# Audio tower on one core: three hand-written orders and the PSUM banks are replaced

## What is computed

```python
h = _L0_tok_ref(x, L0_tok_W, L0_tok_b)
h = h + _L0_attn_ref(_layernorm(h), ...)
    # dots = q k^T / 8; attn = softmax(dots); attn = einsum('bhij,hg->bgij', attn, reattn_w)
    # attn = layernorm over the head axis * ln_g + ln_b; out = (attn v) w_out^T + b_out
h = h + _L0_ffn_ref(_layernorm(h), ...)
    # scores = softmax(x gate^T); the two largest, normalised, weigh relu(x w1 + b1) w2 + b2; plus a shared expert
```

## Time and profile before

| | us |
|---|---|
| median of 3 runs | 638.5 (638.1 to 639.48) |
| the profiled execution: its time | 639.33 |
| the profiled execution: its span | 637.5 |
| PE busy | 606.4 (95%) |
| VectorE busy | 441.2 (69%) |
| ScalarE busy | 402.4 (63%) |
| GpSimd busy | 368.5 (58%) |

### The profile page before, as it was taken

How to read it: one execution, slowest core, us unless ns; L and a number is a source line. 1 busy time by engine, 2 the same in 40 slices (tenths; PEclk the granted TensorE clock), 3 DMA queues, 4 the chain that set the end, 5 groups by cost and what they waited for, 6 DMA issues and landing times.

```text
span 637.5 us, 17017 instructions
## 1 busy us (share of the span) xinstructions
PE 606.4 (95%) x6275; PEld 529.2 (83%) x6275; DVE 441.2 (69%) x1322; ACT 402.4 (63%) x1346; POOL 368.5 (58%) x545
## 2 busy tenths in 40 slices
...
DMA packets 15460, 37.43 MB, mean 59 GB/s; under 512 B 1809, under 2 KB 4241, under 8 KB 15377
## 3 DMA queue, kind: packets, MB, share of 16 engines
...
## 4 chain that ended last, share of the span: by engine, by line
PE 75%; ACT 7%; DVE 7%; POOL 5%; issue 3%; DMA 1%; SPq 0%; ACTq 0%; POOLq 0%; DVEq 0%
PE ps_fill L414 13%; PE ps_fill L416 11%; PE ps_fill L415 11%; PE ps_mix L642 9%; PE ps_dots L630 9%; PE ps_av L650 7%; PE ps_fill L778 6%; PE ps_fill L570 4%; ACT ex L803 3%; DVE aT L1086 3%; POOL sum L1227 2%; PE ps_fill L770 2%; ACT sq L811 2%; POOL sum L1230 1%; PE ps_fill L761 1%
## 5 line engine op out<-in xcount | busy, mean ns | idle before, releaser
L803 ACT ACTIVATE ex<-ps_dots,negmax 128x92 f32<-128x92 f32 x384 | 123.7, 341 | 7.0 <-DVE negmax L1070 6.5
L1227 POOL TENSOR_TENSOR sum<-sq 92x384 f32<-92x384 f32 x64 | 64.2, 1003 | 80.3 <-ACT sq L811 79.5
L1221 POOL TENSOR_TENSOR probs<-ex,rinv 128x552 f32<-128x552 f32 x64 | 71.0, 1109 | 29.7 <-DVE rinv L1076 29.7
L642 PE MATMUL ps_mix<-mixk,probs 64*92 64x64 f32 x1536 | 79.2, 251 | 5.5 <-DVE aT L1086 5.4
L642 PEld LDWEIGHTS ps_mix<-mixk,probs 64*92 64x92 f32 x1536 | 70.7, 163 | 16.3 <-issue 10.7
L1167 DVE SCALAR_TENSOR_TENSOR act<-ps_fill,b_neg,spread 128x368 f32<-128x368 f32 x123 | 67.9, 591 | 19.9 <-PE ps_fill L416 15.1
L803 ACT ACTIVATION_READ_ACCUMULATOR ex<-ps_dots,negmax 128x1 f32 x384 | 81.4, 212 | 0.0
L630 PE MATMUL ps_dots<-xT,yT 128*64 128x92 f32 x1536 | 75.6, 249 | 5.5 <-ACT ex L803 4.9
L630 PEld LDWEIGHTS ps_dots<-xT,yT 128*64 128x64 f32 x1536 | 65.0, 139 | 11.6 <-ACT ex L803 8.8
L1086 DVE TENSOR_TENSOR aT<-ps_mix,arstd 92x384 f32<-92x384 f32 x128 | 64.9, 547 | 7.1 <-ACT arstd L821 5.2
L1244 POOL TENSOR_TENSOR xT<-xT_split_hi,xT_split_lo 128x368 f32<-128x368 f32 x16 | 15.6, 973 | 86.1 <-DVE xT_split_lo L1146 86.1
...
## 6 DMA issues: line engine op xcount, KB each, us to landing
...
```

The lines of the kernel that those rows point to most:

```text
L642: last = pe.matmul(ps_mix[0:N, half, DH * c:DH * c + DH], probs[rows, (s - 1) % 2, c, :], mixk[rows, :, :].rearrange("p g i -> p (g i)"), ...
L803: last = act.activation(ex[:, s % 2, c, :], ps_dots[:, c // HALF, o:o + N], ACT.Exp, bias=negmax[:, c:c + 1], accum_out=sums[:, s % 2, c:c ...
L1221: pool.tensor_tensor(probs[:, s % 2, :, :], ex[:, s % 2, :, :], rinv[:, s % 2, :].unsqueeze(2).broadcast_to([128, CHUNKS, N]), ALU.mult).t ...
L1227: pool.tensor_tensor(sum4[:, :, :, :], sq[:, :, 0:4, :], sq[:, :, 4:8, :], ALU.add)\
```

## The change

The tables STEPS, ORDER_0, ORDERS_END and BANKS get other contents; SETUP has the same contents in another layout of the text. No instruction is added or removed apart from this, and the functions are the same, so lines after the tables stand one lower in number.

```diff
-STEPS = [('dots', 0), ('max', 0), ('av', 0), ('ev', 0), ('mix', 0), ('exa', 0), 'Z5', 'Z3', 'Z2', ('sq', 0), ('exb', 0), 'Z6',
- ('inv', 0), 'XE', ('dots', 1), ('rstd', 0), ('max', 1), ('scale', 0), 'Z8', 'Z0', 'Z1', ('exa', 1), ('mix', 1),
...
+STEPS = [('mix', 0), ('sq', 0), ('dots', 0), ('max', 0), 'XE', ('av', 0), 'Z0', 'XO', ('exa', 0), 'Z2', ('rstd', 0), 'Z1',
+ ('scale', 0), ('exb', 0), ('inv', 0), ('ev', 0), 'H0', 'Z8', 'Z3', 'Z6', ('dots', 1), ('max', 1), ('av', 1),
...
+BANKS = [['Z0', 'Z8', 'OP', 'TH2', 'TX2', 'V2', 'Y4', 'Y0', 'V0'],
+ ['Z1', 'Z6', 'Z7', 'TK', 'TH', 'TX', 'CT', 'BS', 'Y5', 'Y2', 'Y3'],
+ ['Z2', 'Z3', 'Z5', 'Z4', 'V3', 'RT', 'YF', 'Y1', 'Y7', 'Y6']]
...
+ORDER_0 = [('dots', 0), 'shift', ('max', 0), 'XE', 'XO', ('exa', 0), 'prepG', ('exb', 0), 'prepF', 'TK', 'V3', ('dots', 1),
...
- ['Z1', 'Z0', 'Z8', 'T2', 'Z3', 'T4', 'T5', 'T6', 'T7', 'YF']]
+ ['Z8', 'Z3', 'T6', 'Z0', 'Z1', 'T5', 'T2', 'T7', 'T4', 'YF']]
```

More of the change, by code:

```diff
@@ L74 @@
           "av": 2, "ev": 2}
-STEPS = [('dots', 0), ('max', 0), ('av', 0), ('ev', 0), ('mix', 0), ('exa', 0), 'Z5', 'Z3', 'Z2', ('sq', 0), ('exb', 0), 'Z6',
- ('inv', 0), 'XE', ('dots', 1), ('rstd', 0), ('max', 1), ('scale', 0), 'Z8', 'Z0', 'Z1', ('exa', 1), ('mix', 1),
[5 rows of a table removed]
+STEPS = [('mix', 0), ('sq', 0), ('dots', 0), ('max', 0), 'XE', ('av', 0), 'Z0', 'XO', ('exa', 0), 'Z2', ('rstd', 0), 'Z1',
+ ('scale', 0), ('exb', 0), ('inv', 0), ('ev', 0), 'H0', 'Z8', 'Z3', 'Z6', ('dots', 1), ('max', 1), ('av', 1),
+ ('mix', 1), ('ev', 1), 'H1', ('exa', 1), 'Z5', 'Z7', 'OP', ('sq', 1), 'Z4', ('exb', 1), ('rstd', 1), ('dots', 2),
+ 'shift', ('max', 2), ('inv', 1), 'TH2', ('exa', 2), 'TK', ('exb', 2), 'V3', ('scale', 1), ('mix', 2), 'NH2',
[4 rows of a table added]
 LAG = {"XE": 1, "XO": 1, "TK": 1, "TH": 1, "NH": 1, "TX": 1, "BS": 1, "V0": 1, "V2": 0, "V3": 0,
@@ L98 @@
 NBANK = 3
-BANKS = [['Z5', 'Z6', 'Z1', 'TK', 'TH', 'V3', 'TX', 'Y5', 'Y1', 'Y0'],
- ['Z3', 'Z8', 'Z7', 'TH2', 'TX2', 'RT', 'CT', 'Y3', 'Y4', 'V0'],
- ['Z2', 'Z0', 'OP', 'Z4', 'V2', 'YF', 'Y6', 'Y2', 'Y7', 'BS']]
+BANKS = [['Z0', 'Z8', 'OP', 'TH2', 'TX2', 'V2', 'Y4', 'Y0', 'V0'],
+ ['Z1', 'Z6', 'Z7', 'TK', 'TH', 'TX', 'CT', 'BS', 'Y5', 'Y2', 'Y3'],
+ ['Z2', 'Z3', 'Z5', 'Z4', 'V3', 'RT', 'YF', 'Y1', 'Y7', 'Y6']]
 BANK = {step: n for n, steps in enumerate(BANKS) for step in steps}
@@ L130, in present @@
     return exists(G + LAG[step], NG)
[L134 to L146, removed]
[4 rows of a table removed]
+ORDER_0 = [('dots', 0), 'shift', ('max', 0), 'XE', 'XO', ('exa', 0), 'prepG', ('exb', 0), 'prepF', 'TK', 'V3', ('dots', 1),
+ ('inv', 0), ('max', 1), ('mix', 1), ('exa', 1), ('sq', 1), ('exb', 1), 'TH', 'V2', ('dots', 2), ('inv', 1),
+ ('max', 2), ('rstd', 1), ('scale', 1), 'NH', ('mix', 2), ('exa', 2), ('exb', 2), ('sq', 2), ('dots', 3), 'TX',
+ ('rstd', 2), ('max', 3), ('av', 2), ('inv', 2), 'Y4', ('scale', 2), 'Y7', ('exa', 3), 'Y5', 'XS', ('ev', 2),
+ ('mix', 3), ('sq', 3), 'Y3', ('exb', 3), 'Y6', ('inv', 3), 'Y0', ('rstd', 3), 'BS', ('av', 3), 'Y2', ('scale', 3),
+ 'V0', 'Y1', ('ev', 3)]
```

11 lines of the change are left out of this document (7 added, 4 removed), and 16 rows, old and new, of tables (ORDERS_END, STEPS).

## The result

The changed kernel takes **633.39 us** (median of 4 runs, 630.78 to 634.0) where the kernel before takes 638.9 beside it (4 runs, 638.1 to 639.48): ratio 0.9906, 95% interval 0.9884 to 0.9927. That is 0.9% faster; 631.6 was forecast, with 627.0 to 637.5 as the range. The profiled execution took 634.0 us with a span of 632.2; before it was 639.33 and 637.5.

A forecast was written before the change was run, and what follows sets the result against it. PE was taken as the bound, busy 606.4 of 637.5 us. Terms -3.4 (middle) -3.0 (iteration 0) -1.0 (iteration 1) -1.0 (iterations 15, 16) +1.5 (end) = -6.9 us, giving 631.6 us on the median's scale; 8-in-10 range 627.0 to 637.5.

The forecast's parts named there:

- the middle: Iterations 2 to 14: -0.26 us each from a vanished wait for aT and fewer borders, -3.4 us in all (-2.1 to -4.7).
- the end: Last experts: VectorE's second instruction, expert 6, waits for the last spread DMA, so output begins later; +1.5 us (0 to +1.9).
- iteration 0: First iteration: TK fills the wait before dots 1, idle time more scattered, clock may stay up; -3.0 us (-1.2 to -4.6).
- even distance: Middle: mix 3 to next mix 0, and aT to mix 2, came out even; open wait 0 to 0.3 us each, taken 0.
- Rival 2: The wait moves: an even distance in the middle is 0.3 us short per iteration, 3.9 us back, 635.5 us; chance 0.12.
- The number of blocks of small matmuls among the large ones stays six: Middle: block count unchanged, so only one more place where dots and av touch gains, -0.10 us per iteration; transposes taken 0.
- The routing: Middle: shift_l runs clear of probs, VectorE wins up to 0.3 us, but nobody waits for it; costed at 0.
- Rival 3: Slower: routing meets GpSimd's additions, mix waits for late VectorE, 0.9 us per middle iteration, 643.3 us; chance 0.10.
- Iteration 1: Second iteration: about 7.5 us of waiting, before dots 1 and CT, instead of 8.5, clock falling twice; -1.0 us (-3 to +2).
- Iterations 15 and 16: Wait before av 3 becomes waits of about 2 us before mix 0 and av 1 of iteration 16; -1.0 us (-2.5 to +1.5).
- Rival 1: The clock eats the edges: falls in iterations 0 and 16 make the edges +1.8 us, 636.9 us in all; chance 0.14.
- Rival 4: Whole kernel: same matmuls, PE 95% busy, waits and losses only change places, 637.5 to 639.5 us; chance 0.08.

The follow-up runs named there:

- split_clean: The changed kernel with Z5 moved from behind mix 1 to between av 1 and mix 1, in STEPS alone; 635.92 us, ratio 0.9970.
- last_order: The changed kernel with the last iteration's list rewritten so VectorE takes experts in the order the spread DMAs are issued; 628.01 us, ratio 0.9844.
- tail_busy2: The changed kernel with ten unread matmuls ahead of the first wide expert (T6) of the last iteration, timed a second time; 629.73 us, ratio 0.9848.
- setup_y: The changed kernel with Y5 and Y4 exchanged in the list of the setup; 631.25 us, ratio 0.9896.

## Why the prediction was right, and where it was not

The direction and the range were right, and most of the waits came as forecast. The sizes of the middle and of the end were not, and the total came near because they miss in opposite directions. The range had a slip of its own: the middle at -4.7 and iteration 0 at -4.6 make 628.7 us, not 627.0. Step by step:

- **The wait of mix 1 for `aT`** (-0.16 forecast): gone in all 13 iterations, and neither even distance turned into a wait of PE. Rival 2 is out.
- **"The number of blocks of small matmuls among the large ones stays six"; "[I] take 0"** for transposes. This term was mis-sized: 0.10 us forecast for the borders, some 0.4 measured. I counted blocks of small matmuls and did not look at the runs of large ones where transposes stand at a border. In iteration 8 the 27 matmuls of the Z steps stood in four runs (12, 9, 3 and 3) and now stand in three (18, 6 and 3); one run of three stood between two transposes. Over all kinds there were eight runs of full matmuls and are now seven, if the six short ones of RT count as a border. Measured from start to start, the Z steps went from 5.46 to 5.00 us, of which 0.15 is the wait of the earlier trace rows and 0.2 a run less, by split_clean; the transposes went from 1.77 to 1.62, dots from 4.25 to 4.11 (-0.10 forecast), RT from 0.75 to 0.69; V, TK, Y and BS together took back 0.26. The sum is the 0.57 us by which iteration 8 is shorter (0.59 in the mean of the 13), against 0.26 forecast. The bound of 0.10 for transposes was too narrow. The 0.1 us that is left of the Z steps, and the transposes' 0.15, were not tested by themselves.
  The Trainium skill has a rule (TensorEngine Tiling (Array Packing), Key Properties): changing the tiling mode drains TensorE. The trace agrees so far as each border between small and full matmuls costs about 0.1 us, a price that the page does not give. But the rule is not the whole: the same 0.27 us from the first to the second matmul of a run stands where all the matmuls near use the whole array of 128 x 128, behind RT in iteration 8 of the kernel before (332.21 to 332.48) and behind the wait in last_order (616.64, shown above, to 616.91). So the price of a run is shown, and what makes it is open. The rows, of the kernel before and then of last_order:

```profile
332.21 0.44 PE L761 MATMUL ps_fill<-combT,b_all 128*128 128x368 f32 x1
332.48 1.09 PE L778 MATMUL ps_fill<-act,w_sb 128*128 128x368 f32 x3
```

```profile
616.91 0.33 PE L414 MATMUL ps_fill<-x2T_lo,w_split_hi 128*128 128x368 f32 x1
```

- **The routing** (0 forecast). `shift_l` takes 0.23 us in each of the middle iterations, before 0.52, and PE waits for nothing there either way. VectorE had slack, so this part of the change was worth nothing that a measurement shows. Rival 3 is out too: an addition does hold `shift_l` (last section), but by 0.04 us.
- **Iteration 0** (-3.0, "about 25.5 us"): 26.4 in one profile, 25.53 at full clock in the other. Waits of 0.3, 0.9, 1.9 and, together, 0.7 us lie near the forecast 0.4, 1.1, 1.9 and 1.0. Right, and so was the doubt: the profiles have its clock from 1.00 down to a low stretch of 10.2 us.
- **Iteration 1** (-1.0): both waits are as forecast (3.1 and 4.2 us). The term cannot be read from one profile. It was +0.8 in one and -4.4 in the other, with the same waits.
- **Iterations 15 and 16** (-1.0): -1.8. The wait before av 1 is 1.8 us as forecast, and the one before av 3 stayed, 1.5 us. Mix 0 waits 0.2 and not 2: the eight matmuls of KEEP_BUSY stand ahead of it (583.44 to 585.04), and I had left them out. Only one low stretch of 3.4 us came.
- **The end** (+1.5): +4.2. At full clock it is +1.6 (18.53 us against 16.90 in tail_busy2), so the forecast was right as long as the clock stayed up, and by its own pieces: expert 6 starts 10.34 us after CT, behind the last landing at 10.31. What I missed is that expert 3 waits for the second DMA and starts 1.8 us later than experts 0 and 1 before. This does not move expert 6, but YF starts later by it. The step that failed is the one not taken: a later start of YF makes PE's hole longer (1.61 us before, 3.92 after), and the clock fell in it, at 619.35. I let the clock fall in iterations 0, 1 and 16 and did not ask it of the end.
- **The setup** (nothing forecast): +1.6, of it 0.9 by the bank table (setup_y); 0.35 was there before the first Y (16.94 us against 16.59; this start lies anywhere from 16.64 to 17.32 in the other profiles), and the rest stays open. The list of the setup is unchanged, so I did not cost it; but its banks are new.
- **Rival 1** (the clock eats the edges) came true in size rather than in place: it took some 2.6 us at the end, and up to 5 in iteration 1. **Rival 4** (nothing but order, 637.5 to 639.5) is out by the time.
